# Sending each token to its two experts in sorted tiles of 128 rows, in place of computing all experts for all tokens

## The reference

```
x = x + attn(layernorm(x))              # A: causal, 8 query heads of 128, one key and value head
x = x + xattn(layernorm(x), ctx)        # B: 16 heads of 16, a 256x256 bias for each head and a mask
x = x + ffn(layernorm(x))               # C:
    logits = x @ gate_w.T;  the two best of 8 experts by logits + lb_bias
    w = sigmoid(logit of each of the two), divided by their sum
    expert_out[e] = square(relu(x @ w1[e].T)) @ w2[e].T          # 256 -> 256 -> 256
    out = w[first] * expert_out[first] + w[second] * expert_out[second]
        + square(relu(x @ cfc.T)) @ cproj.T                      # the shared expert
```

## Time and profile before

| | |
|---|---|
| median of 3 runs | 2559.81 us (2558.17 to 2561.91) |
| profiled execution, own time | 2559.14 us |
| its span, first to last instruction | 2557.4 us |
| mean granted TensorE clock | 0.991 |

### The profile page before, as it was taken

The page is one execution under the profiler, slowest core; times in us unless marked ns, Lnnn a source line. Parts: engine busy times, 40 slices in busy tenths (PEclk is TensorE's granted clock), DMA queues, the critical chain, the costliest instruction groups (busy, mean ns, idle before and its releaser), DMA issues.

```text
span 2557.4 us, 77106 instructions
## 1 busy us (share of the span) xinstructions
PE 2340.5 (92%) x26176; PEld 2036.7 (80%) x26176; DVE 2007.8 (79%) x6672; ACT 2060.2 (81%) x6065; POOL 1788.1 (70%) x1899
## 2 busy tenths in 40 slices
PE   4789999999999999999999999999999999999987
PEld 3678888888888888888888888888888888888876
DVE  5578788778788778788778788778788778788765
ACT  6777888877888877888877888877889877889864
POOL 2566677866677866677866677866677766677764
PEclk9899999999999999999999999999999999999999
DMA  5232222232222232222232222232222232222230
GB/s 167 92 105 87 92 86 89 84 109 86 92 88 89 84 109 82 96 87 90 84 109 81 96 86 91 85 109 80 94 87 93 84 109 80 93 88 93 80 100 10
DMA packets 171126, 233.14 MB, mean 91 GB/s; under 512 B 20720, under 2 KB 119280, under 8 KB 170736
## 3 DMA queue, kind: packets, MB, share of 16 engines
q1 hardware_dynamic: 170736, 228.21, 27.4%
HBM read 202.98 MB, written 25.17 MB: 89 GB/s over the span
## 4 chain that ended last, share of the span: by engine, by line
PE 63%; DVE 13%; ACT 11%; issue 10%; POOL 3%; DMA 1%; SPq 0%; DVEq 0%; ACTq 0%; POOLq 0%
PE ps_c_out L955 10%; PE ps_c_hidden L955 10%; PE ps_a_misc L955 9%; PE ps_b_probsT L1083 8%; PE ps_b_misc L1097 3%; PE ps_b_misc L955 3%; PE ps_b_scores L1071 3%; PE ps_a_scores L1009 3%; PE ps_a_misc L1028 2%; DVE b_neg_scores L817 2%; POOL bias L510 2%; DVE a_qT L769 2%; PE ps_b_probsT L955 2%; PE ps_b_scores L955 2%; PE ps_a_probsT L1016 1%
## 5 line engine op out<-in xcount | busy, mean ns | idle before, releaser
L510 POOL TENSOR_TENSOR bias<-bias,b_mask 128x512 f32<-128x512 f32 x512 | 646.9, 1278 | 0.0
L817 DVE CUSTOM_DVE_ANT_0 b_neg_scores<-ps_b_scores,bias 128x256 f32<-128x256 f32 x1024 | 391.7, 419 | 95.3 <-PE ps_b_scores L1071 34.8
L531 POOL TENSOR_TENSOR c_hidden_lo<-c_hidden,c_hidden_hi 128x512 f16<-128x512 f32 x288 | 334.2, 1160 | 131.2 <-ACT c_hidden_hi L683 90.8
L825 DVE TENSOR_TENSOR b_probsT_lo<-ps_b_probsT,b_probsT_hi 128x512 f16<-128x512 f32 x512 | 352.7, 689 | 63.6 <-ACT b_probsT_hi L660 53.7
L1083 PE MATMUL ps_b_probsT<-constants,b_probs 128*128 128x128 f32 x2048 | 323.3, 281 | 29.1 <-DVE b_probsT_lo L825 15.1
L524 POOL TENSOR_TENSOR c_hidden<-c_relu 128x512 f32<-128x512 f32 x288 | 300.3, 1043 | 56.3 <-ACT c_relu L678 55.2
L660 ACT ACTIVATE b_probsT_hi<-ps_b_probsT 128x512 f16<-128x512 f32 x512 | 303.1, 592 | 24.8 <-PE ps_b_probsT L1083 20.0
L955 PE MATMUL ps_c_out<-w_hi,c_hidden_hi 128*128 128x256 f16 x1152 | 314.3, 273 | 5.0 <-DVE acc L926 2.7
L955 PE MATMUL ps_c_hidden<-c_xT_hi,w_hi 128*128 128x256 f16 x1152 | 314.6, 273 | 3.7 <-ACT c_relu L678 2.3
L955 PE MATMUL ps_c_hidden<-c_xT_hi,w_lo 128*128 128x256 f16 x1152 | 314.8, 273 | 0.0
L955 PE MATMUL ps_c_hidden<-c_xT_lo,w_hi 128*128 128x256 f16 x1152 | 314.7, 273 | 0.0
(11 more groups left out here) (198 smaller groups left out, 8333.5 us busy)
## 6 DMA issues: line engine op xcount, KB each, us to landing
bias<-in_bias SPq DMA_DIRECT2D x256, 512.0 KB, 3.5
q_stack<-qk_scratch SPq DMA_DIRECT2D x256, 64.0 KB, 2.4
x_ln<-in_x SPq DMA_DIRECT2D x32, 256.0 KB, 2.8
ctxT<-in_ctx SPq DMA_DIRECT2D x32, 256.0 KB, 3.6
x_res<-in_x SPq DMA_DIRECT2D x32, 256.0 KB, 4.0
qk_scratch<-b_kT_hi_lo SPq DMA_DIRECT2D x32, 256.0 KB, 2.3
k_stack_even<-qk_scratch SPq DMA_DIRECT2D x128, 64.0 KB, 2.4
k_stack_odd<-qk_scratch SPq DMA_DIRECT2D x128, 64.0 KB, 2.4
```

The lines of the kernel that those rows point to most:

```text
L510: gp.tensor_tensor(part, part, b_mask[:, :], ALU.add).then_inc(b_c_ok, 1)
L531: gp.tensor_tensor(c_hl[:, u, :], c_h[:, :], c_hh[:, u, :], ALU.subtract).then_inc(c_h_ok, 1)
L817: last = dve.tensor_tensor_reduce(out=b_t[:, u, c, :], in0=ps_bs[:, c * T:(c + 1) * T], in1=bias[:, slot, at:at + T], scale=-2.0, scalar=3 ...
L825: dve.tensor_tensor(b_pTl[:, j % 2, :, :], ps_bpt[:, :].rearrange("p (c t) -> p c t", c=CT), b_pTh[:, j % 2, :, :], ALU.subtract).then_inc ...
```

## The change

1. **Routing.** Batches are taken in groups (seven of 4, two of 2). After the gate, PE counts with matmuls against a triangle of ones and a matrix of ones how many earlier tokens of the group chose each expert (`c_rank`); DVE makes from it, once a group, a table that says which expert each tile of 128 rows belongs to (`c_table`, 9 instructions), and for each batch the two rows of every token (`c_pos`). A group of 4 batches has `4*2*2 + 8 = 24` tiles, whatever the routing, a group of 2 has 16: 200 tiles in all. A tile that an expert doesn't fill is computed all the same.
2. **Rows through DRAM.** The normalised rows, split into float16 parts of `2*256` values, are written by four indirect DMAs of POOL a batch into a buffer in DRAM, sorted by expert. For each tile SP loads the 128 rows back transposed (`dma_start_transpose`, 128 KB), reads the tile's expert from the table into a register, and loads that expert's split weights (512 KB) into one of two slots. Results (128 KB a tile) are stored to DRAM, and four indirect DMAs of POOL a batch fetch each token's two rows. DVE adds them with the gate's weights to the value that waited in DRAM, and SP stores the output.
3. **A tile** is 12 matmuls of 128 columns, relu and square on ACT (128x256), square and lower part on POOL (128x256), 6 matmuls of 256 columns, and one copy out of PSUM by DVE (128x256).
4. **Shared expert** dense as before, once a batch. The c transposes on PE go: SP transposes the split rows by a DMA from SBUF (`c_xT`).
5. **Banks.** q, k, v of stage B and the transposed x of stage B now pass through `ps_c1`, one after another, in place of `ps_bm`, `ps_bpt` and `ps_bs`; experts' tiles use the halves of `ps_c2`.
6. **Weights.** The split weights of the eight experts are written to DRAM at the start; the first loads of weights are spread over the first iterations. Three row buffers in DRAM are zeroed at the start.
7. **Orders** are new. The tiles of batches 0 to 19 run in 6 a batch, from iteration 11 on PE (A runs two to three iterations behind i, B three to four, C five, tiles eleven to twelve). The last 80 tiles stand at iterations of their own: on PE tiles up to 24 are in the iterations of the last batches' A and B, the other 55 come after the last step of stage B. From the 25th of the 80 on, tiles also use the banks of stage A.

```diff
-W20 = W10 + NX * CD * HID
+W20 = W10 + CD * HID
+GRP = 4
+TILES = GRP * CT * 2 + NE
+PER = TILES // GRP
+GROUPS = [GRP] * (BATCHES // GRP - 1) + [GRP // 2] * 2
+TAIL = 5
+ANCHOR = 24
+SETS = 3
-LAGS = 3
+LAGS = 24
...
+        def hidden_bank(tile):
+            if tile < TILE0[TAIL + 1]:
+                return ps_c2[:, 0:2 * P]
+            return (ps_as if tile % 2 == 0 else ps_apt)[:, 0:2 * P]
...
+            def m_load_x(b, k):                                    # SP
+                tile, group = numbered(b, k)
+                sp.wait_ge(m_sc[group % SETS], scattered(group))
+                sp.wait_ge(m_f1_ps, max(tile - 1, 0))
+                at = (tile - TILE0[group]) * P
+                sp.dma_start_transpose(m_x[:, tile % 2, :, :], row_d[group % SETS][at:at + P, :])...
+            def m_load_w(b, k):                                    # SP
+                sp.wait_ge(g_tb, TAB_STEPS * (group + 1))
+                sp.wait_ge(m_f2_ps, max(tile - 1, 0))
+                expert = sp.value_load(m_tab[0:1, at:at + 1], min_val=0, max_val=NE - 1)
+                sp.dma_start(m_w[:, tile % 2, :, :]..., wt_d[bass.DynSlice(expert, 1), :, :]...)
+            def m_store(b, k):                                     # SP
+                sp.wait_ge(m_y_ok, tile + 1)
+                sp.dma_start(y_d[group % SETS][at:at + P, :], m_y[:, tile % 2, :])...
+            def m_shared(b, _):                                    # SP
+                sp.wait_ge(s_out, 16 * b)
+                sp.dma_start(x_out[:, :, :], xs_d[b])...
...
-            def c_f1(b, e):                                        # POOL, nine a batch
-                gp.tensor_tensor(c_h[:, :], c_r[:, e % 2, :], c_r[:, e % 2, :], ALU.mult)
+            def c_f1(b, _):                                        # one a batch
+                gp.tensor_tensor(c_r[:, :], c_r[:, :], c_r[:, :], ALU.mult)
+            def m_square(b, k):                                    # POOL, each tile
+                gp.tensor_tensor(m_h[:, :], m_r[:, tile % 2, :], m_r[:, tile % 2, :], ALU.mult)
+            def m_lo(b, k):
+                gp.tensor_tensor(m_hl[:, tile % 2, :], m_h[:, :], m_hh[:, tile % 2, :], ALU.subtract)
+            def m_scatter(b, n):                                   # POOL, four a batch
+                gp.indirect_dma_start(row_d[group % SETS], IndirectOffsetOnAxis(m_pos...), c_rows[:, b % RING, c, :, :]...)
+            def m_gather(b, n):                                    # POOL, four a batch
+                gp.indirect_dma_start(m_yg[:, c, choice, :], None, y_d[group % SETS], IndirectOffsetOnAxis(m_pos...))
...
+            def m_relu(b, k):                                      # ACT, each tile
+                act.activation(m_r[:, tile % 2, :], hidden_bank(tile), ACT.Relu, scale=R_UP / W_UP)
+            def m_sq(b, k):
+                act.activation(m_hh[:, tile % 2, :], m_r[:, tile % 2, :], ACT.Square)
...
-                    last = dve.scalar_tensor_tensor(out=acc[:, c, :], in0=ps_c2[:, c * D:(c + 1) * D],
-                                                    scalar=g_we[:, c, e - 1:e], in1=acc[:, c, :], ...)
+            def m_evict(b, k):                                     # DVE, each tile
+                dve.tensor_copy(m_y[:, tile % 2, :], out_bank(tile))
+            def m_combine(b, choice):                              # DVE, two a batch
+                for c in range(CT):
+                    last = dve.scalar_tensor_tensor(out=x_out[:, c, :], in0=m_yg[:, c, choice, :],
+                                                    scalar=g_w12[...], in1=x_out[:, c, :], ...)
+            def c_pos(b, part):                                    # DVE, five instructions a batch
+                ... one add, two products, one reduce, one cast to integers
+                # c_gate gets parts 13 to 15: one subtract, two products, one reduce
...
+            def c_rank(b, _):                                      # PE, 8 columns each
+                    for n, (e, ec) in enumerate(earlier):
+                        pe.matmul(ps_c1[:, at:at + NE], ones[:, :], g_m[:, e % RING, ec, :], ...)
+                    last = pe.matmul(ps_c1[:, at:at + NE], before[:, :], g_m[:, b % RING, c, :], ...)
+            def m_f1(b, k):                                        # PE, 12 matmuls of 128 columns
+                pe.wait_ge(m_x_ok[u], 16 * (tile // 2 + 1))
+                pe.wait_ge(m_w_ok[u], 16 * (tile // 2 + 1))
+                for m in range(2):
+                    last = pair_product(hidden_bank(tile)[:, m * P:(m + 1) * P], ...)
+            def m_f2(b, k):                                        # PE, 6 matmuls of 256 columns
+                pe.wait_ge(m_h_ok, tile + 1)
+                last = pair_product(out_bank(tile), ...)
```

751 lines of the change are left out of this document (584 added, 167 removed).

## The result

The changed kernel is slower: 2741.2 us (median of 4 runs, 2737.3 to 2747.4) against 2559.3 of the kernel before, a ratio of 1.071, 95% interval [1.0686, 1.0737]. Forecast were 2486, 2320 to 2650.

A forecast was written before the change was run, and what follows sets the result against it. PE was taken to bound the kernel before, DVE after; fill 136 + 10, periods 7 x 63 + 24 x 67.3, last batch's C 10, tail 248 + 24 gave 2484 us of span, 2486 in all, range 2320 to 2650.

The forecast's parts named there:

- PE sets the period: Steady periods before the change: PE busy 72.3 of 76.6 us, 9 us ahead of the next engine.
- I keep this share: 63.5 / 0.944 = 67.3: Steady periods after: DVE leads with 63.5 us and reaches PE's old busy share of 0.944, so 67.3 us a period.
- The loads: Busy time per steady period after the change: DVE 63.5, PE 59.5, ACT 58.3, POOL 56 us.
- The 0.8 us taken off for fewer collisions with POOL: DVE's period: less elementwise work on POOL should shrink collisions with SBUF-only instructions, 64.3 to 63.5 us.
- so I add nothing for it: Tail: PE is mostly idle and its granted clock had been 0.89 in the last 46 us; 0 us added.
- Rival 2: Steady periods: POOL becomes the bound through its indirect DMAs; 2670 us at 3.5 us each, chance 0.15.
- X: POOL's time for one of eight indirect DMAs a batch: taken as 1.5 us, bounds 0.2 and 3.5.
- Rival 3: Tail: SP loads one tile's weights after another's, 55 x 6.5 = 358 us, so 2596; decides from 5.8 a tile, chance 0.12.
- The slot loop: Tail: two weight slots, each reloaded only after its tile's second product, some 8 us for two tiles; 4.5 a tile taken.
- the estimate of 5.2 us: Transposing load of a tile's rows, four blocks at the skill's 1309 ns; up to 27 us in the tail.
- the 10 us: Fill: zeros (9.4 MB, 29 us) stand before loads on the same DMA engines; 10 us added, 0 to 30.
- Rival 1: Steady periods: PE still sets the period, 63 us, 59 early, tail 3 us a tile; 2270 us, chance 0.25.

The follow-up runs named there:

- e17: Kernel before the change, one of three matmuls kept in most expert products, 120 matmuls (12.8 us of TensorE a period) fewer: period 79.7 us, 2.9 longer.
- e18: Kernel before the change, one of three matmuls kept only in later experts' products, 72 matmuls (7.7 us a period) fewer: period 76.87 us.
- e9: Changed kernel without most routed weight loads, all scatters and gathers, and the addition of experts' results (a cheap step instead): 2570.9 us, period 66.7.
- e4: Changed kernel, only SyncE's order behind the last attention changed to rows, weights, store per tile: 36 us slower in the whole, 23 of it behind the last b_out.
- e14: e13 plus 12 unread filler matmuls ahead of each first product from the tail's 41st tile on: 312.4 us behind the last b_out for 308.2.
- e13: Changed kernel with three weight slots for two, loads one tile further ahead, six c_rows slots and the tail order of e4: 2720.7 us.
- e3: Changed kernel, the three zero-filling DMAs moved from SyncE iterations 1, 2 and 7 to 4, 5 and 6: first b_out at 187.5 us.
- e11: Changed kernel, only experts 0 and 1 split and stored, the others get copies, first bias loads wait for ten pieces: 10 us less fill.
- e8: Changed kernel with four slots for the routed tiles' output in place of two, and six c_rows slots for eight: periods 73.56 us.
- e6: Changed kernel without scatters and gathers, GpSimd only counting the semaphores up: 2639.9 us.

## Why the prediction was wrong

- **The step that failed: "PE sets the period", and from it "I keep this share: 63.5 / 0.944 = 67.3".** It was mis-sized by 6.3 us in 24 periods, 151 of the miss of 257 in the span. A busy share of 0.944 was read as a bound. But TensorE runs the experts' matmuls where attention makes it wait, and e17 and e18 take 12.8 and 7.7 us of them away and gain nothing. So the share was filled up by these matmuls and not a bound, and it did not come over to the new leader: VectorE has 0.85 after, and the highest share in e9 is 0.90.
- **The loads were forecast well, and did not decide.** From the second window, times 73.6: TensorE 61.7 us a period (59.5 forecast; at half clock twelve matmuls of 128 columns took 1.44 us, e4 at 2595.07, for 0.83 at full clock), VectorE 62.3 (63.5), ScalarE 59.0 (58.3), GpSimd 54.0 (56). On VectorE errors cancelled: combining costs 4.1 us and not 1.6, the two gate products 2.5 and not 0.8, and the rows' lower parts (mean 1.47 us, line below) were not counted, while they replace a step of 0.7. Against that all small steps of gate, positions and table, these products included, came to 10.9 us a period (the fifteen from the ninth on), for the 9.8 of before and 5.4 added; a cast costs 0.24 and not 1.02. The 0.8 us taken off for fewer collisions with POOL had the wrong sign for the combining steps.

```profile
L1285 DVE TENSOR_TENSOR c_rows<-c_xn,c_rows 128x512 f16<-128x512 f32 x32 | 47.0, 1468 | 47.4 <-ACT c_rows L1011 47.4
```

- **"so I add nothing for it", of the clock,** said of the tail and left out of the periods. In the tail the clock was 0.60, not the 0.89 of before, and yet nothing had to be added (e14). The periods have 8.9 us each at half clock, which at the slopes of 0.3 to 0.6 would be 2.7 to 5.3 us of the 6.3, an estimate; but e4 has 5.7 and the same period. So what the clock took stays open. The drops go with waits that the matmuls had filled (e17).
- **The holds.** The miss is spread: weights' transfers 1.6, indirect DMAs 2.5, combining 1.5 us a period, which together bring the period back to the forecast (e9), perhaps in part through the clock (half-clock time 8.9 to 2.5). How much of each is the hold itself and how much the drop behind it stays open. The forecast had these loads in its sum, but nothing for what they do to the steps behind them.
- **Rival 2, POOL and its indirect DMAs,** was nearest in mechanism and had 0.15. Its condition, X above 2.4 us, was not met: X is 0.98 and 0.99 in the two groups. POOL was the most loaded engine in none of the three windows; its time counts all the same, 7.6 us of it being worth 4.3 after (with VectorE's gain) and 0.8 before. By the estimate that the Trainium skill (SBUF — State Buffer, section SBUF: two separate sides) led to, X would have been 3.1; no issue lasted over 1.23 us. Its other half, that VectorE's and GpSimd's SBUF steps shut each other out, the traces agree with, at a higher price than I took: 1013 ns for 408, and 600 with fewer of GpSimd's additions.
- **Rival 3, the tail:** 337 us behind the last b_out, where its price would have given 392 and mine 282; the 58 tiles still to be evicted then took 5.4 us each, below its 5.8. The slot loop was the right mechanism (e13); per pair it is 10.2 us in e4 for the 8 that I had and the 9 that I took. I had allowed 1 us a slot for all of SyncE's issues and reads; a transpose alone holds it 1.2 us, and weights wait behind it. A tile's rows need 3.7 us from the start of their issue to the first product (e13, 2634.01 to 2637.72), so the estimate of 5.2 us, from the figure in the Trainium skill, VectorE: DVE Perf Modes, section The three transpose paths, is too long here.
- **Fill:** the 10 us were put on the zeros, which cost nothing (e3). 40 came: 10 from the weights' staging (e11), and for the rest perhaps the added iteration between self- and cross-attention, which the orders show, no run tests, and I had not looked for.
- **Rival 1** (2270) needed TensorE to be what is short; e18 shows that in the kernel before it was not.

## What to carry to other kernels

Before removing work from the busiest engine, look at what ends the waits around that work: here matmuls that filled waits for other engines gave nothing back when they went, and in e17 gaps and half-clock stretches came in their place. Take the same amount out of the kernel before and time it: here such a run gave no gain at all. And where four engines in fixed order have 0.69 to 0.86 each, price every hold by a run: weights, indirect DMAs and combining cost 1.5 to 2.5 us a period each, which the busy sums do not show, and the wait for stores (e8) nothing.

## What the runs showed of the hardware

- A step of VectorE with two SBUF inputs can be held over a row of back-to-back GpSimd steps: a product of 128x16 took 4.17 us beside four of them (1.14 to 1.30 us each, at 903.16 us), 2.36 in the mean, and 0.16 in e6, where it falls clear of them. In combining the two engines alternate: four steps, 0.47 us at the least, took 5.74 beside five bias additions.
- An indirect DMA of 128 rows held GpSimd 0.94 to 1.22 us (means 0.98 and 0.99), with 0.3 us to the next. A transposing load of rows held SyncE 1.22 us in the median of 200 (1.19 to 2.69), a load of weights 0.35 (0.34 to 1.12).
- 2.4 us of idle TensorE among work were followed by 3.4 us at half clock (e17); the kernel before, where no wait of TensorE's in its periods is above 1.54 us, kept the full clock. A long gap is not needed: e18 has none above 1.54 us either, and fell for 6.8 us at 1445 us, behind matmuls with gaps of 0.5 to 1.1.
